# Who subtracts the low halves of the normed rows: GpSimd, or VectorE between the shared slots' work

## The reference, cut to what matters

```python
# attention-like term: adj is the layer norm of x
xij = sigmoid(si[:, :, None] + sj[:, None, :] + b)      # si, sj: ctx @ W halves
x = x + tanh(g_xattn) * (0.6 * xij + 0.4 * layernorm(x))
# mixture of experts on the normed rows
h = layernorm(x)
probs = softmax(h @ gate_w.T); top 4 of 16, weights renormed
out = sum over chosen experts of w * (swiglu(h @ W_gu[e]) @ W_dn[e])
out = out + swiglu(h @ Ws_gu) @ Ws_dn                    # the shared expert, all rows
x = x + tanh(g_ffn) * out
```

## Time and profile before

| | |
|---|---|
| median of 3 runs | 690.98 us (688.97 to 691.63) |
| the profiled execution | 689.59 us, its span 687.8 us |
| PE busy | 622.2 us (90%) |
| DVE busy | 495.9 us (72%) |
| ACT busy | 325.5 us (47%) |
| POOL busy | 339.1 us (49%) |
| L461 on POOL | 16 subtractions, median 1202 ns, first at 35.8 and last at 118.6 us |

### The profile page before, as it was taken

The page is one execution under the profiler, slowest core; times in us unless marked ns, Lnnn a source line. Parts: engine busy times, 40 slices in busy tenths (PEclk is TensorE's granted clock), DMA queues, the critical chain, the costliest instruction groups (busy, mean ns, idle before and its releaser), DMA issues.

```text
span 687.8 us, 17262 instructions
## 1 busy us (share of the span) xinstructions
PE 622.2 (90%) x4394; PEld 376.7 (55%) x4395; DVE 495.9 (72%) x1271; ACT 325.5 (47%) x558; POOL 339.1 (49%) x510
## 2 busy tenths in 40 slices
PE   3768869877898999999999999999999999999992
PEld 2444546445555566565655656565665656566561
DVE  6978788989676758687788767688588878767110
ACT  1763667331343454554445455454555544454541
POOL 2631844115234465555546555564655646565432
PEclk9999989998999999999999999999999999999997
DMA  8670111119156876758587684948767587644532
GB/s 233 220 228 2 62 46 63 48 41 286 51 156 146 201 172 141 170 126 184 111 210 164 143 210 82 227 74 202 175 136 175 118 202 160 148 89 78 91 38 41
DMA packets 49841, 93.72 MB, mean 136 GB/s; under 512 B 8840, under 2 KB 16776, under 8 KB 49816
## 3 DMA queue, kind: packets, MB, share of 16 engines
q0 software_dynamic: 16128, 38.35, 30.0%
q1 hardware_dynamic: 32936, 55.04, 27.4%
q10 hardware_dynamic: 752, 0.04, 0.1%
HBM read 65.16 MB, written 28.24 MB: 136 GB/s over the span
## 4 chain that ended last, share of the span: by engine, by line
PE 74%; DVE 10%; ACT 4%; DMA 4%; POOL 3%; issue 2%; SPq 1%; DVEq 0%; POOLq 0%; ACTq 0%
PE gu_ps L1208 43%; PE bank L1236 20%; PE bank L1248 4%; PE bank L1222 4%; DMA dn_sc<-dn_scale_halves 2%; DMA room_a<-in_ctx 1%; PE gu_ps L1168 1%; DVE act L995 1%; POOL mix_room L495 1%; ACT acth L626 1%; DVE X L1004 1%; DVE acth L1000 1%; PE bank L1165 1%; POOL room_a L461 1%; ACT mix_room L585 1%
## 5 line engine op out<-in xcount | busy, mean ns | idle before, releaser
L1208 PE MATMUL gu_ps<-wgu,mix_room 128*128 x1728 | 305.1, 326 | 3.4 <-DVE tick L954 2.1
L1208 PEld LDWEIGHTS gu_ps<-wgu,mix_room 128*128 128x128 f16 x1728 | 166.2, 98 | 115.1 <-issue 8.0
L1236 PE MATMUL bank<-wdn,aT 128*128 (+1 forms) x792 | 185.3, 379 | 4.2 <-ACT aT L633 3.7
L534 POOL DMA_INDIRECT out<-mix_room,idx_s x72 | 122.7, 1705 | 32.0 <-issue 30.9
L633 ACT ACTIVATE aT<-bank 128x768 f16<-128x768 f16 x88 | 71.2, 810 | 136.9 <-PE bank L1222 132.1
L1236 PEld LDWEIGHTS bank<-wdn,aT 128*128 128x128 f16 x792 | 77.3, 98 | 88.9 <-issue 2.2
L505 POOL TENSOR_TENSOR pool_tick<-ones 128x1 f32<-128x1 f32 x144 | 35.8, 249 | 163.4 <-DMA out<-mix_room,idx_s 86.4
L995 DVE SCALAR_TENSOR_TENSOR act<-gu_ps,wslot,sg x72 | 44.5, 617 | 96.4 <-ACT sg L619 84.4
L626 ACT ACTIVATE acth<-act 128x384 f16<-128x384 f32 x88 | 46.0, 523 | 128.2 <-DVE act L995 128.2
L516 POOL DMA_INDIRECT room_b<-token_rows,idx_g x72 | 76.9, 1067 | 12.2 <-issue 3.7
L1000 DVE TENSOR_TENSOR acth<-act,acth (+1 forms) x88 | 51.1, 580 | 38.2 <-ACT acth L626 37.8
(11 more groups left out here) (157 smaller groups left out, 594.6 us busy)
## 6 DMA issues: line engine op xcount, KB each, us to landing
dn_sc<-dn_scale_halves SPq DMA_DIRECT2D x34, 384.0 KB
dn_raw<-in_L_ffn_down_packed SPq DMA_DIRECT2D x48, 256.0 KB
gu_sc<-gu_scale_halves SPq DMA_DIRECT2D x34, 192.0 KB
X<-in_x SPq DMA_DIRECT2D x4, 1024.0 KB, 8.1
token_rows<-room_a SPq DMA_DIRECT2D x16, 256.0 KB, 2.0
out<-X SPq DMA_DIRECT2D x4, 1024.0 KB, 11.6
gu_raw<-in_L_ffn_gate_up_packed SPq DMA_DIRECT2D x16, 192.0 KB
gu_raw<-in_L_ffn_gate_up_packed SPq DMA_DIRECT2D x16, 191.9 KB
```

Of the source, the lines that this page charges most:

```text
L534: nc.gpsimd.indirect_dma_start(out[:, :], bass.IndirectOffsetOnAxis(idx_s[:, b:b + 1], 0), y_sb[:, b, :], None, compute_op=ALU.add).then_i ...
L1208: mm = nc.tensor.matmul(ps[b][:, 0:I], x(xp * HC + c), wgu[:, w, wp, c, col:col + I], start=(c == 0 and xp == 0 and wp == 0), stop=(c == H ...
L1236: mm = nc.tensor.matmul(y_ps[0 if shared else b][:, :], aT[:, b, ap, t, :], wdn[:, w, wp, t, :], start=(n == 0), stop=(n == 3 * IC - 1))
```

## The change

GpSimd keeps the subtractions of tiles 0 to 3. Those of tiles 4 to 15 become VectorE instructions in `after_shared_slot`: tiles 4 and 5 at the end of slot 2's part, 6 and 7 at the end of slot 3's, 8, 10, 12 and 14 at the end of slots 4 to 7, and 9, 11, 13 and 15 at the head of slots 5 to 8's. `LEAD` goes from 68 to 44.

```diff
-        LEAD = 68
+        LEAD = 44
...
             inverse_std(1, 1)
             norm_factors(1)
-            low_halves_x(1)
...
             norm_factors(2)
-            low_halves_x(2)
             inverse_std(1, 3)
             norm_factors(3)
-            low_halves_x(3)
...
+            def low_x(k):
+
+                v.wait_ge(xn_ready, k + 1)
+                v.wait_ge(xh_ready, k + 1)
+                nc.vector.tensor_tensor(xhl[:, k % ROWS_AHEAD, 1, :], xn[:, k % 2, :], xhl[:, k % ROWS_AHEAD, 0, :],
+                                        ALU.subtract).then_inc(xl_ready, 1)
+
             def after_shared_slot(i):
 
+                if 4 < i <= NT // 2:
+                    low_x(2 * i - 1)
                 if i == 2:
                     first_stats(2)
                     first_stats(3)
...
                 if i in (7, 8):
                     first_weights(i - 5)
+                if i in (2, 3):
+                    low_x(2 * i)
+                    low_x(2 * i + 1)
+                if 4 <= i < NT // 2:
+                    low_x(2 * i)
                 if i == 9:
                     route()
```

## The result

The changed kernel takes 712.99 us (median of 4 runs, 711.29 to 714.06) against 691.11 us (median of 4 runs, 688.97 to 691.63), 21.9 us more; the ratio is 1.032, interval 1.029 to 1.035. The forecast was 710.2. The profiled execution took 713.09 us, its span is 711.3 against 687.8: 23.5 us more.

A forecast was written before the change was run, and what follows sets the result against it. Between 67 and 130 us the chain runs through all four engines, VectorE carrying slots 5 to 9. Delays of 3.5 + 5.7 + 3.4 + 8.0 = +20.6 us on the profiled 689.59 gave 710.2 us, range 703 to 716.

The forecast's parts named there:

- A: Slot 2 to 3: tiles 4 and 5 stand behind statistics of batches 2 and 3; +3.5 us, +3.0 without a clock fall.
- B: Slot 3 to 4: tile 6 stands behind attend and statistics of batch 2; +5.7 us, +4.1 without a clock fall.
- C: Slot 4 to 5: tile 8 stands behind attend and statistics of batch 3; +3.4 us, +1.8 without a clock fall.
- D: Slots 5 to 8: odd tiles wait behind the previous output's addition, even tiles behind dequantising; 40.9 against 32.9 us, +8.0.
- rival 4: More clock falls in slots 5 to 8 (two, 3.2 us) and a lost port race or two: 714 to 717 us; chance 0.13.
- The race for the port: Tiles 4, 6, 8: the urgent subtraction starts before GpSimd's power operation, adding nothing; three lost races up to 3.1 us.
- Nothing behind slot 9 takes it up: After slot 9 the routing steps move as a whole, so the entire shift reaches the end.
- The fills: Kernel start: removing 24 leading fills gains nothing, since VectorE's first real work waits 3.84 us for a DMA after them.
- Rival 1: The clock holds in some or all of slots 2 to 5: 706.5 us; chance 0.25.
- Rival 3: Only one half of the delay comes, from slots 3 to 5 or 5 to 8: 698 to 702 us; chance 0.09.
- Rival 5: VectorE's or GpSimd's loop code moves and fetches elsewhere: some us either way, held inside the range; no separate chance.
- Rival 2: Ending GpSimd's hold-up of VectorE is worth more than TensorE's waiting: 685.5 us, faster; chance 0.03.

The follow-up runs named there:

- e3: Changed kernel plus 22, 29, 14 and 4 unread matrix products before TensorE's waits for tiles 4, 6, 8 and 12; 707.44 us.
- e8: Changed kernel with LEAD, the number of leading fills, put back from 44 to 68; 714.46 us.
- e1: Changed kernel with only tiles 4 to 7 subtracted by VectorE, tiles 8 to 15 by GpSimd as before; 700.37 us.
- e2: Changed kernel with only tiles 8 to 15 subtracted by VectorE, tiles 4 to 7 by GpSimd as before; 703.70 us.
- e4: Changed kernel with two places of slots 5 to 7 exchanged: even tile right behind the addition, next odd tile at the slot's end; 702.28 us.
- e5: e4 with the remaining VectorE subtractions moved to earlier places too, so all twelve stand early; 687.44 us.
- e6: Kernel before the change, all subtractions on GpSimd, with only the iota moved to GpSimd's first idle time; 688.15 us.
- e9: e7 with the subtractions of tiles 4 to 7 back on GpSimd (LEAD 52); 686.11 us.
- e10: e9 plus ten unread matrix products before the transposes of tile 8; 687.59 us.
- e7: e5 and e6 together: all twelve subtractions early on VectorE, iota in GpSimd's first idle time; 687.78 us.

## Why the prediction was right, step by step

The forecast was +20.6 us against the profiled execution; it was +23.5 (and +21.9 between the medians). The mechanism was the one foreseen; two terms were too small, A's and D's. By its own steps:

- **A**, +3.5 (3.0 without a fall of the clock): measured 14.46 less 10.31, +4.15. The place was right (transposes at 74.32, forecast 74.20). The clock's price was mis-sized: I took 1.59 us from a stretch in which it rose part of the way; here nearly all of gate and up ran at the lower level (1.2 GHz), 3.96 against 2.11 us, and transposes to activation took 5.45 us for the 4.80 foreseen. With the clock held (e3) the distance grew by 3.02 us, and there it is ScalarE's path that ends last, as foreseen: from its held-up copy at 73.59 to the activation at 77.92 it takes 4.33 us (4.30 foreseen).
- **B**, +5.7: measured +5.97. **C**, +3.4: measured +3.37; attend took 2.73 us, as foreseen. The reason given was wrong: the 3.63 us of before was not beside GpSimd's scaling, which had ended before attend began at 89.30 (the row below), but beside the subtraction of tile 8 at 91.15. That subtraction went with the change, so the 0.90 came all the same.

```profile
78.61 8.12 POOL L444 TENSOR_SCALAR X<-X,lnA,lnB 128x512 f32<-128x512 f32 x8 [1.97 <-DVE lnA L752]
```

- **D**, +8.0: measured +9.67. Slots 5, 7 and 8 took 9.64, 11.04 and 8.94 us (9.8, 11.1 and 8.9 foreseen). Slot 6 took 12.95 instead of 11.1: the two fills that were left out (0.46 us from 127.63 to 128.09) and a fall of the clock at 129.51, the one thing of rival 4 that came. e3 takes that fall away and the slot takes 11.61.
- **The subtraction itself**, 0.68: measured 0.68 to 0.69, and 1.29 for two in a row. **The race for the port:** the urgent subtraction won every time, and GpSimd's power operation waited (1.36 us at 105.52 instead of 1.01; 1.39 behind tiles 4 and 6). Three lost races by rows of 1.01 us would have been 3.0 us, not 3.1:

```profile
105.52 1.36 POOL L438 TENSOR_TENSOR rstd<-veps,mhalf 128x4 f32<-128x4 f32 x1 [11.80 <-DVE veps L729]
```

- **Nothing behind slot 9 takes it up:** 23.2 of 23.5 us had come by the activation of slot 9. **The fills:** nothing up to slot 9, as e8 shows.
- **Rival 1** (full clock) is what e3 made: 707.4 for the 706.5 foreseen. **Rival 3** (one half only) fell: both halves came, and e1 and e2 give each by itself. Of **rival 4** one fall came and no lost race. **Rival 5** (the place of the code) left no trace up to slot 9 in e8; behind it, it stays open. **Rival 2** (the hold-up is worth more than the waiting) failed for the change as made, by the condition the prediction gave; e4 meets that condition for slots 5 to 8 and there gains 2.9 us, e5 for all and gains 3.4 in the total (685.5 was foreseen, 687.4 measured). Its size was too high for two reasons that the rows show: of slot 6's 2.45 us that were "not work", 0.46 are the two fills (113.18 to 113.64), and in slot 5 there is nothing to gain, since TensorE's own queue needs 7.49 us for it (the same in the kernel before and in e4, where VectorE waits 0.99 us).

What the Trainium skill's page "SBUF — State Buffer" says under "Who interferes with whom" (whoever starts first holds the shared port pair for the whole instruction) agrees with the 2.65 us that became 0.35 in e6. For the power operation it agrees in who waits; the 0.35 us it lost are somewhat less than the 0.46 that the subtraction still had to run. It says what a hold-up costs, not whether it is on the path: e1 has GpSimd's hold-ups in slots 5 to 9 and is 12.6 us faster than the kernel without them.

## What to carry to other kernels

When work moves to an engine with time to spare, look first at its place in that engine's queue, and then at its duration: here twelve instructions of 0.68 us cost 22 us behind statistics and additions, and in earlier places (e5) the kernel was 3.4 us faster than before. For each consumer write down when its own queue reaches the wait, and put the producer ahead of everything that this consumer doesn't need; where a loop runs through both engines (down, addition, subtraction, transposes), take the next item's work from the end of the slot before. And look for long operations with no inputs on a shared port, like the iota here: moving it alone to an idle time gave 2.7 us in the total and 2.2 in the distances, most of what the best of these kernels gained.

## What the hardware showed that was not expected

The fall of the granted clock isn't a fixed function of one gap. After 2.97 us of idle time the transposes of tile 4 ran at full clock in the kernel before (0.64 us) and at the lower level in e9 and e10 (1.04 us after 2.98); after 2.11 us the first routed gate and up took 2.12 or 3.18 us. e5 and e7 differ in the same way after 3.66 us. Once down, twelve products of gate and up took 3.0 to 4.05 us instead of 2.11. What that costs a slot depends on what else it waits for: 1.1 to 1.8 us where e3 took the fall away, and nothing in slot 2 to 3 of e9, which took 10.33 us with the fall and 10.31 in the kernel before without it. Each subtraction of GpSimd beside attend held it up by 0.90 us: 2.73 us with none (e2), 3.63 with one, 4.53 with two (e1).
